# Hyperbolic attention in one fused program: inverses of the softmax sums with queries on partitions, and four logarithms in another place

## The reference

```python
dist = jnp.arccosh(jnp.maximum(-inner, 1.0 + 1e-06))      # inner: hyperbolic products of q and k
scores = (1.0 - alpha) * scores_euclid + alpha * (-(dist * dist) / curv_k)
scores = jnp.where(causal[None, None], scores, -jnp.inf)
attn = jax.nn.softmax(scores, axis=-1) * spike_mask       # spike_mask: 0 or 1 for each query
y = jnp.einsum('bhts,bhsd->bhtd', attn, v)
y = jnp.transpose(y, (0, 2, 1, 3)).reshape(B, T, C)
```

## Time and profile before

| | us |
|---|---|
| median of 3 runs | 2808.99 (2806.58 to 2811.42) |
| the profiled execution | 2812.88 |
| its span on the core | 2811.0 |
| the hyperbolic stage, first matmul to last VectorE instruction | 1559.0 to 1662.7 |

### The profile page before, as it was taken

The page is one execution under the profiler, slowest core; times in us unless marked ns, Lnnn a source line. Parts: engine busy times, 40 slices in busy tenths (PEclk is TensorE's granted clock), DMA queues, the critical chain, the costliest instruction groups (busy, mean ns, idle before and its releaser), DMA issues. The chain is left out here.

```text
span 2811.0 us, 38689 instructions
## 1 busy us (share of the span) xinstructions
PE 2357.8 (84%) x15016; PEld 1377.6 (49%) x15016; DVE 1502.4 (53%) x2414; ACT 1047.6 (37%) x1874; POOL 300.6 (11%) x595
## 2 busy tenths in 40 slices
PE   2999999778998798999995866866879799698778
PEld 1344444335797463444443542432227657365447
DVE  4778777332221457888863862337986433223433
ACT  2566666412110234777772641213212233021310
POOL 2453000000000300000001510100000000000100
PEclk8899999987999897999997677876778899888889
DMA  6977443010453897555420001001004440200200
GB/s 188 244 184 168 92 91 61 26 69 1 180 225 129 258 279 187 95 121 98 92 30 33 12 1 58 28 1 61 0 0 150 154 161 1 92 3 0 99 0 8
DMA packets 108214, 258.60 MB, mean 92 GB/s; under 512 B 11808, under 2 KB 83072, under 8 KB 94080
## 3 DMA queue, kind: packets, MB, share of 16 engines
q1 hardware_dynamic: 101696, 203.71, 27.5%
q0 software_dynamic: 2736, 39.37, 4.1%
q10 hardware_dynamic: 3600, 13.04, 1.2%
HBM read 211.26 MB, written 44.83 MB: 91 GB/s over the span
## 5 line engine op out<-in xcount | busy, mean ns | idle before, releaser
L666 DVE TENSOR_REDUCE sta_parts<-sta_psA 128x1 f32<-128x1024 f32 x544 | 625.8, 1187 | 188.3 <-PE sta_psA L583 186.6
L724 ACT ACTIVATE sta_probs<-sta_psS 128x512 f32<-128x512 f32 x1056 | 575.9, 597 | 274.8 <-PE sta_psS L594 272.8
L594 PE MATMUL sta_psS<-L_xattn_qS,L_xattn_kst 99*128 99x256 bf16 x2112 | 356.3, 278 | 11.4 <-ACT sta_probs L724 6.6
L583 PE MATMUL sta_psA<-L_xattn_kst,L_xattn_qS 99*128 99x512 bf16 x1088 | 293.3, 387 | 46.9 <-PEq L59 32.1
L594 PEld LDWEIGHTS sta_psS<-L_xattn_qS,L_xattn_kst 99*128 99x128 bf16 x2112 | 161.4, 98 | 259.4 <-ACT sta_probs L724 183.1
L603 PE MATMUL sta_psO<-sta_probs,L_xattna_V 128*32 128x256 f32 x2560 | 189.5, 385 | 0.0
L583 PEld LDWEIGHTS sta_psA<-L_xattn_kst,L_xattn_qS 99*128 99x128 bf16 x1088 | 104.3, 99 | 131.7 <-DVE sta_parts L666 43.8
L202 ACT ACT_TABLE_LOAD x14 | 18.0, 1283 | 339.0 <-PEq L59 339.0
L2357 PE MATMUL l2t_psY<-l2t_hc,top_consts_weights 128*128 128x512 f32 x128 | 93.5, 845 | 30.7 <-DVE l2t_hc L2393 30.6
L603 PE MATMUL sta_psO<-sta_probs,L_xattn_V 128*32 128x256 f32 x1536 | 114.8, 390 | 0.0
L1008 ACT ACTIVATE sht_probs<-sht_psS 128x768 f32<-128x768 f32 (+1 forms) x64 | 55.3, 863 | 152.8 <-PE sht_psS L852 101.3
(11 more groups left out here) (617 smaller groups left out, 3973.5 us busy)
## 6 DMA issues: line engine op xcount, KB each, us to landing
L_xattn_kst<-L_xattn_keys SPq DMA_DIRECT2D x186, 136.0 KB, 5.0
L_xattn_kst<-L_xattn_keys SPq DMA_DIRECT2D x186, 128.0 KB, 4.6
L_xattn_values<-prj_rows SPq DMA_DIRECT2D x64, 256.0 KB, 3.7
L_xattn_keys<-prj_parts SPq DMA_DIRECT2D x32, 384.0 KB, 4.0
L_xattna_V<-in_ctxV SPq DMA_DIRECT2D x5, 2048.0 KB, 11.8
L_xattna_V<-L_xattn_values SPq DMA_DIRECT2D x5, 2048.0 KB, 11.0
l2f_W<-in_M SPq DMA_DIRECT2D x10, 1024.0 KB, 7.6
L_xattn_keys<-sta_bparts SPq DMA_DIRECT2D x24, 384.0 KB, 8.2
```

What stands on the lines that cost most here:

```text
L583: last = nc.tensor.matmul(psA[:, u % 2, col:col + rhs.shape[1]], lhsT, rhs, start=True, stop=True)
L594: last = nc.tensor.matmul(psS[:, at % 2, j * T:(j + 1) * T], lhsT, rhs, start=True, stop=True)
L666: nc.vector.tensor_reduce(into(parts[:, u // n % 2]), view(psA[:, u % 2, :]), AX.X, ALU.max).then_inc(max_taken, 1)
L724: nc.scalar.activation(probs[:, u % NP, i * 512:(i + 1) * 512], psS[:, at % 2, :], ACT.Exp, scale=scale).then_inc(probs_ready, 1)
```

## The change

Four things are changed, all in `hyperbolic_softmax`.

1. The spikes are no longer spread over the partitions at the start: the four matmuls L1955 and the copy L2072 are gone.
2. The inverse of a sum is made with queries on partitions. `sums(g)` on TensorE takes the four sums of each query out of `yP` with two small matmuls (128 x 4 each) into the upper half of the bank of `psY`. `invert(g)` on VectorE takes the reciprocal of 128 x 8 numbers and multiplies by the spikes, which lie with queries on partitions anyway. `widen(g)` on ScalarE copies each inverse 32 times (128 x 256). `spread(g)` on TensorE turns that back with two matmuls (128 x 128 each) into `psN`. `scale(g)` on VectorE multiplies `psN` by `yP` into `attT`.
3. `psY` and `psN` are now single: `values(g)` also waits until `invert(g - 1)` has read its sums (`inverse_in`), and `spread(g)` waits for `widen(g)` and for `scale(g - 1)`.
4. The logarithms of pairs 8 to 11 (batch 1) stand ahead of the exponential of pair 4, within the weights of batch 0. Those of pairs 12 to 15 stay between the two batches.

```diff
                def values(g):
                     pe.wait_ge(turn_copied, 2 * g + 2)
                     if g:
                         pe.wait_ge(y_copied, g)
+                        pe.wait_ge(inverse_in, g)
...
+                def sums(g):
+                    pe.wait_ge(y_copied, g + 1)
+                    for t in range(TB):
+                        last = nc.tensor.matmul(psY[:, T + 4 * t:T + 4 * t + 4], yP[:, g % 2, t * P:(t + 1) * P], K["col32"], start=True, stop=True)
+                    last.then_inc(sums_ready, 1)
+
+                def spread(g):
+                    pe.wait_ge(widened, g + 1)
                     if g:
-                        pe.wait_ge(inverted, g)
-                    else:
-                        pe.wait_ge(spikes_copied, 1)
-                    nc.tensor.matmul(psN[:, g % 2, :], K["sel32"], yP[:, g % 2, :], start=True, stop=True).then_inc(spread_ready, 1)
+                        pe.wait_ge(scaled, g)
+                    for t in range(TB):
+                        last = nc.tensor.matmul(psN[:, t * P:(t + 1) * P], wide[:, g % 2, t * P:(t + 1) * P], K["ident"], start=True, stop=True)
+                    last.then_inc(spread_ready, 1)
...
                         turn(k)
                         if k % 2 == 0 and k > first:
                             values(k // 2 - 1)
+                        if k % 2 == 0 and k > first + 2:
+                            spread(k // 2 - 2)
                         if k % 2 and k > first + 1:
-                            spread_sums((k - 3) // 2)
+                            sums((k - 3) // 2)
                     values(end // 2 - 1)
-                    spread_sums(end // 2 - 1)
+                    spread(end // 2 - 2)
+                    sums(end // 2 - 1)
+                    spread(end // 2 - 1)
...
+                def invert(g):
+                    b = g // (QUADS // B)
+                    dve.wait_ge(sums_ready, g + 1)
+                    V.reciprocal(inverse[:, g % 2], psY[:, T:T + 4 * TB].rearrange("p (t h) -> p t h", t=TB)).then_inc(inverse_in, 1)
+                    dve.wait_ge(inverse_in, g + 1)
+                    V.tensor_tensor(inverse[:, g % 2], inverse[:, g % 2], spikes[:, b * TB:(b + 1) * TB].unsqueeze(2).to_broadcast([P, TB, 4]),
+                                    ALU.mult).then_inc(inverted, 1)
...
-                        if k % 2 and k >= first + 5:
-                            normal((k - 5) // 2)
-                    normal(end // 2 - 2)
-                    normal(end // 2 - 1)
+                        if k % 2 == 0 and k >= first + 4:
+                            invert(k // 2 - 2)
+                        if k % 2 == 0 and k >= first + 6:
+                            scale(k // 2 - 3)
+                    invert(end // 2 - 2)
+                    scale(end // 2 - 3)
+                    scale(end // 2 - 2)
+                    invert(end // 2 - 1)
+                    scale(end // 2 - 1)
...
                     for k in range(first, end):
+                        if b + 1 < B and k == first + HALF // 2:
+                            logarithms(range(end, end + HALF // 2))
                         act.wait_ge(top_ready, k + 1)
...
                             if k % 2 and k > first + 1:
                                 copy_y((k - 3) // 2)
+                            if k % 2 and k >= first + 5:
+                                widen((k - 5) // 2)
                     copy_turned(end - 1)
+                    widen(end // 2 - 2)
                     copy_y(end // 2 - 1)
+                    widen(end // 2 - 1)
```

## The result

The changed kernel takes 2829.29 us, median of 4 runs (2826.68 to 2835.67), against 2807.78 before: a ratio of 1.0079, 95% interval 1.0066 to 1.0092. It is **21.5 us slower**. The forecast was +9, with a range that ended at 2824: the direction was right, the size was less than half of it, and the time lies outside the range.

A forecast was written before the change was run, and what follows sets the result against it. The prediction took a ring of waits among ScalarE, TensorE and VectorE to bound the stage. Start -1.06, batch 0 with boundary +5.1 to +8.9, batch 1 +2.85 to +6.95 made +9, 2818 us, range 2812 to 2824.

The forecast's parts named there:

- The mechanism: Within the batches, the ring of one pair ahead becomes one long chain through all three engines: +2.5 to +6.3 in batch 0.
- The chain from `widen(0)` to `widen(1)`: Steps on TensorE, VectorE and ScalarE: 2.96, 3.15 and 2.75 us at full clock; TensorE's 5.0 at half.
- The start: At the first hyperbolic matmul: the spike matmuls ahead of it go and all that follows comes earlier, -1.06 us.
- the table loads: On ScalarE around the logarithms: 1.30 us per switch; rival with the skill's cost, +2.8 on the forecast, 2821, chance 0.03.
- the boundary: Between the batches on ScalarE: four logarithms less give 3.36 us back.
- The step that failed first: In the sum: 0.78 of the time at 2.4 GHz gives +8.6, a little more for TensorE standing still, +9.
- the half-clock sum: All terms with TensorE at 1.2 GHz throughout the chains: +14.8 us, against +6.9 at 2.4 GHz.
- the last stretch: End of the chain in each batch, from `spread(1)` through values to `widen(3)`: 4.9 us at full clock, 6.6 at half.
- Up to exponential 13: In batch 1: `invert(4)` stands ahead of scores 13, its sums behind turn 11, +1.45 us.
- A sign that failed with it: In the profile after: first exponential of batch 1 comes 4 to 8 us later than 1631.04.
- The early rise of the clock in batch 1: Rival: spreads and sums keep TensorE's clock up, three pairs gain 3.9 us, time 2814; chance 0.14.
- the waits are met in time: Rival: `widen(0)` and `widen(1)` are done when TensorE comes to the spreads, sum -6.2, time 2803; chance 0.07.

The follow-up runs named there:

- e3 to e6: Changed kernel with spreads later (2819.2 us), small reciprocals later (2817.3), both later (2812.7), both later and logarithms back between the batches (2809.2).
- e3: Changed kernel with TensorE's spreads of quads 0, 1, 4, 5 moved behind the turn of the next odd pair: 2819.2 us.
- e6: Changed kernel with both the spreads and the small reciprocals moved later and all eight logarithms back between the batches: 2809.2 us, ratio 0.9996.
- e7: Changed kernel with useless matmuls filling TensorE's idle time, no wait taken away: 2822.8 us, and 2820.1 when run again.
- the changed kernel again: The changed kernel, nothing edited, executed and profiled once more: 2828.7 us.
- e11: Changed kernel with a second copy of each widened inverse, into a tile nothing reads, ahead of each widening copy on ScalarE: 2832.9 us, one run.

## Why the prediction was wrong in size

Term by term, the profiled changed kernel (126.0) against the profiled kernel before, from ScalarE's rows above and the earlier trace rows:

| stretch | before | after | measured | forecast |
|---|---|---|---|---|
| stage's start to exponential 4 | 46.72 | 52.06 | +5.3 | +4.9 |
| exponential 4 to the table load | 15.99 | 24.65 | +8.7 | +2.5 to 6.3 |
| to exponential 8 | 9.33 | 6.02 | -3.3 | -3.4 |
| to exponential 13 | 15.60 | 19.71 | +4.1 | +1.45 |
| to the end | 16.10 | 23.54 | +7.4 | +1.4 to 5.5 |
| sum | 103.74 | 125.98 | +22.2 | +6.9 to 14.8 |

- **The mechanism was right.** TensorE stands at `spread` for `widen`, VectorE at `invert` for `sums`, ScalarE before exponentials 7 and 15 and before copies 5 and 13. The forecast waits at the first spread (1.7) and second (over 3) were 0.80 and 3.14. The first was shorter because turn 4 and the values ahead of it ran at half clock. e3 to e6 show that these two places are the largest part of the loss, 10.8 us at equal clock, and the clock behind them the next. The chain from `widen(0)` to `widen(1)` had been priced at 2.96 + 3.15 + 2.75 = 8.9 us at full clock and 10.9 at half, and took 9.22 and 11.52.
- **The start, the table loads and the boundary were right.** VectorE starts 0.96 us behind the stage's first matmul instead of 2.03. A switch is 1.30 us here too, and the dearer one of the Trainium skill (ScalarE: Activation LUTs, What ACT_TABLE_LOAD costs), 2.66, is not seen again: the row at 1611.98 has its exponential at 1613.28.
- **The step that failed first is the one where I picked the clock.** I let the chains run 0.78 of the time at 2.4 GHz, because the same stretches before did, and added 0.4 us for more standing still. I treated the clock as given, though the change makes TensorE stand still. The granted clock was 0.52 and 0.60 from 1616 on, and it rose to 0.78 when e7 filled the standing time. e7 prices this at 4.6 to 9.0 us where I had added 0.4. In my own sum the choice is worth 14.8 - 9 = 5.8 of the 13.2 us that were missing in the profiled stage (22.2 against 9). Both ends of my range should have come from the chain with its own clock, and the half-clock sum was the likelier end. The range's lower end has a slip as well: 2808.99 + 6.9 is 2815.9 and not 2814.7, which moves nothing here.
- **The half-clock sum was itself 7.4 us short**, of which some 4 were in the chains. From exponential 4 to the load it was 24.65 where I had 22.3, and from exponential 13 on 23.54 where I had 21.6. I had priced `spread` at 0.7 us at half clock; it holds TensorE for 1.02 (1.22 with its end). I had left `spread(2)` out of the last stretch, though it stands ahead of `sums(3)`. I had also left out the new wait of `values` on the single bank. The trace puts waits of 0.39 us down to it, twice. But ScalarE's copy of the turned weights, which the values need too, ended at 1633.52, and the reciprocal at 1633.58, so the bank itself cost under 0.2 us each time:

```profile
1632.72 0.80 ACT L2064 COPY hyp_R<-hyp_banks 128x768 f32<-128x768 f32 x1 [2.59 <-PE hyp_banks L1931]
```

```profile
1633.37 0.21 DVE L1999 RECIPROCAL hyp_inverse<-hyp_psY 128x8 f32<-128x8 f32 x1 [6.02 <-PE hyp_psY L1951]
```

```profile
1633.72 1.51 PE L1943 MATMUL hyp_psY<-hyp_R,l1a_v 128*32 128x256 f32 x16 [0.39 <-DVE hyp_inverse L1999]
1635.16 1.22 PE L1959 MATMUL hyp_psN<-top_consts_weights,hyp_wide 128*128 128x128 f32 x4
1636.18 0.85 PE L1951 MATMUL hyp_psY<-top_consts_weights,hyp_yP 128*128 128x4 f32 x4
```

- **Up to exponential 13 I let the half-clock case change nothing but the chains.** Before, the granted clock went from 0.50 to full between 1642.4 and 1642.8, 11 us into batch 1, and exponentials 12 to 13 went at full clock; after, it stayed low: +4.1 where I had +1.45, 2.65 us of the 7.4.
- **A sign that failed with it.** Exponential 8, to be 4 to 8 us late, was 10.7 us late counted from the stage's start (82.73 us into it against 72.04).
- **The rivals.** The early rise of the clock in batch 1 (14%) went the other way. That the waits are met in time (7%) failed where it was said to decide: at `spread(0)` TensorE was there first.

What stays open: why the same changed kernel has a stage of 126.0 us in one profile and 121.6 in the other. The clock rows say that its rises fell in other places, not why.

## What to carry to other kernels

Before an instruction is put into an in-order queue, ask what stands behind it there, and whether what it waits for has itself to pass another engine's queue: two such waits that face each other cost up to 10.8 us here at equal clock, and 4.6 to 9.0 more by the clock, with 15 us less work on VectorE. Moving both by one pair in the order, with nothing else changed, gave 15 to 20 us back. Here the waits also lowered TensorE's clock, so a chain that has grown should be costed at 1.2 GHz first and the higher clock be argued for, not the reverse. And where most of a program is not touched, compare the touched stage in two profiles of each kernel: it showed 3 us here (e6, one profile), where the times of 12 runs could not. That holds as far as the stage repeats: 0.1 us for the kernel before, 4.4 for the changed one.

## What the runs showed that I had not expected

- The filled kernel: 36 more matmul records from 1616 to the stage's end (366 against 330), and 4.6 to 9.0 us less stage, by a clock of 0.78 instead of 0.52 or 0.60.
- `invert` waited for GpSimd. A product of 128 x 8 numbers took 1.29 us when GpSimd was squaring, and 0.17 elsewhere. In the three other profiles in which it began under GpSimd's first square it took 1.33, 1.32 and 1.31 us (the changed kernel again, e3 and e11). Timelines of VectorE and GpSimd, changed kernel:

```profile
1609.76 1.29 DVE L2001 TENSOR_TENSOR hyp_inverse<-hyp_inverse,l1a_spikes 128x8 f32<-128x8 f32 x1
```

```profile
1609.56 2.89 POOL L2048 TENSOR_TENSOR hyp_R<-hyp_D 128x768 f32<-128x768 f32 x2 [3.42 <-ACT hyp_D L2060]
```

  It ended at 1611.05, when GpSimd's first square of 1.4 us was done. The logarithms in the middle brought that square to this place; ScalarE was still at them, so it cost nothing here. The Trainium skill (SBUF — State Buffer, Who interferes with whom) says that a VectorE instruction with two inputs in SBUF contends with a GpSimd instruction that reads SBUF, and that the one that comes second is blocked for the whole of the first. The trace agrees: the product has two such inputs and ended with GpSimd's square, while the scores behind it, with one input from PSUM, took their usual 1.38 us beside the next squares.
